# A perceiver block on Trainium2: first cross attention joined with the norm of its latents, and its 33 tail keys on two 64-row halves of TensorE

## The chip, the cores and the metric

One Trainium2 chip, one of its cores (core 0). A kernel's time is that of one launch of the whole program on the device, in microseconds. The kernel before took 2004.42 us in the median of three runs (2004.2 to 2007.45). Its profile is of a further execution, of 2006.4 us.

## The reference, cut to what matters

The program is a two-layer perceiver block in float32: cross attention, gated recurrence, a feed-forward layer, a second cross attention, self attention and a mixture of experts, each on a residual stream `x` of 128 batches x 32 latents x 128 features. The change touches the first cross attention alone:

```python
def _L0_xattn_ref(x, latents, mask, g1, b1, g2, b2, Wq, Wkv, Wout):
    heads, dim_head = (16, 64)
    xn = layer_norm(x, g1, b1)                 # context: 128 batches x 257 rows x 128
    ln_lat = layer_norm(latents, g2, b2)       # latents: 128 batches x 32 rows x 128
    q = ln_lat @ Wq
    kv = jnp.concatenate([xn, ln_lat], axis=1) @ Wkv    # 257 + 32 = 289 keys
    ...
    weight = jnp.where(full_mask, einsum('bhld,bhnd->bhln', q * scale, k * scale), neg)
    weight = softmax(weight)
    out = einsum('bhln,bhnd->bhld', weight, v)
    return out @ Wout
x = x + _L0_xattn_ref(ctx_1024, _layernorm(x), mask, g1, b1, g2, b2, Wq, Wkv, Wout)
```

So each batch has 289 keys: 256 context rows, the last context row, and its 32 latents. The last 33 are the *tail keys*. The latents are normalised twice, once outside and once by `layer_norm(latents, g2, b2)`.

## The kernel before

Stages follow one another, each a block of programs for the five engines (PE, DVE, ACT, POOL and SP, which issues the loads), with a barrier between blocks: `setup`, then `xattn0` (the stage of the change), and five more. Within a block the order of each engine's work is written out by hand, and engines meet at semaphores.

`xattn0` has three blocks. **First**, `ln_stats` (L74 to L133) makes mean and inverse deviations of all latents on DVE, with two square roots on ACT. **Second**, `xattn0_inputs` (L448) goes over the latents in 8 chunks of 512 rows, two buffers deep. For a chunk, DVE and ACT each normalise two of its four 128-row tiles (L480, L528), PE turns the four (L513), ACT copies the turned chunk into `latT` with gain and offset (L534), DVE multiplies by the gain (L486), POOL adds the offset (L501) and SP stores the chunk in DRAM (L557), from where it comes back as values. The last context rows go the same way at the end (`tailT`). **Third**, the attention proper. POOL first clears buffers (L681 to L686, all of `blocks` among them) while DVE, PE and SP wait for `zeroed`.

The attention runs in steps, one a batch, unrolled 8 deep (`run_steps`). Weights are folded: `A` takes the turned latents to queries in context space for each head, and `U` takes a head's weighted context to the output. In step s the engines work ahead by different distances. DVE takes statistics of batch s+7 (L755) and normalises s+6 (L762); POOL applies gain and offset (L694, L696); PE turns batch s+5 (L907), ACT and DVE split it into two float32r parts (L838, L786). PE makes queries for four heads (L879), ACT and DVE split them (L834, L773). PE makes the scores of batch s+3 for four head groups, three float32r products each (L853); DVE masks them and takes the largest (L728), ACT takes the exponentials (L801), DVE the inverse sums (L778). For batch s+2 ACT scales the probabilities (L809) and DVE turns them in 32x32 blocks, 256 keys in one instruction (L739), the tail keys in another (L741); SP then moves the blocks in four transfers so that keys lie on partitions (`probT`, L648), once PE is done with that buffer. For batch s PE makes the values: per 128 keys two float32 products of 256 columns, one for each pair of head groups (L863, two key tiles), then the same for the tail keys (L870). A float32 product is two records in the trace. ACT copies the result out (L819). Every fourth step PE projects the four finished batches with 16 products (L895), and DVE adds them to `x` (L782). A *tile* is four batches.

The tail keys' values lie in `a_tail`, 8 batches deep, on the 128 partitions: latent c on partition 4c, the last context row on partition 1, zeros elsewhere. SP loads a tile's tail in two transfers (L665, L667) every fourth step, and the product at L870 runs over all 128 rows. `LEAD` is 7: before the first batch there are seven steps, -7 to -1, in which only the work ahead is done.

Of the kernel before, what the change touches and what calls it, by code (L numbers as in the profile page):

```python
# [25 lines left out]
P = 128  # L26
# [47 lines left out]
def ln_stats(k, stack, name, extra=None):  # L74
# [11 lines left out]
    with nc.Block() as block:  # L86
# [41 lines left out]
        @block.scalar  # L128
        def _(act):
            for n, root in enumerate((rstd,) if extra is None else (rstd, twice)):  # L130
                act.wait_ge(inv_ready, n + 1)
                nc.scalar.activation(root[:], inv[:], ACT.Sqrt).then_inc(root_ready, 1)
    return (mean, rstd) if extra is None else (mean, rstd, twice)  # L133
# [314 lines left out]
def xattn0_inputs(k, io, stack):  # L448

    nc = k.nc
    k.latT = stack.enter_context(nc.sbuf_tensor("latT", [P, TOK], F32))
    k.tailT = stack.enter_context(nc.sbuf_tensor("tailT", [P, B], F32))
    with ExitStack() as st:
        z2 = st.enter_context(nc.sbuf_tensor("lat_z2", [P, 2, 4, D], F32))
        lat = st.enter_context(nc.sbuf_tensor("lat_affine", [P, 2, 4, D], F32))
        tail = st.enter_context(nc.sbuf_tensor("ctx_tail_affine", [P, 2, D], F32))
        bank = [st.enter_context(nc.psum_tensor(f"lat_ps{u}", [P, CH], F32)) for u in range(2)]
        tail_ps = st.enter_context(nc.psum_tensor("lat_ps_tail", [P, P], F32))
        z2_ready, z2_act, turned, copied = k.sem("lat_z2_ready"), k.sem("lat_z2_act"), k.sem("lat_turned"), k.sem("lat_copied")  # L460
        offset, offset_ready = st.enter_context(nc.sbuf_tensor("lat_offset", [P, TILES], F32)), k.sem("lat_offset_ready")
        scaled, affine_ready, stored = k.sem("lat_scaled"), k.sem("lat_affine_ready"), [k.sem(f"lat_stored{u}") for u in range(2)]
        tail_z, tail_scaled, tail_turned, tail_stored = (k.sem(f"ctx_tail_{n}") for n in ("z", "scaled", "turned", "stored"))
        spread = lambda a: a[:].unsqueeze(1).broadcast_to([P, 4, D])
        k.latents_stored = [(tail_stored, 16)] + [(sem, 16 * CHUNKS // 2 + 16) for sem in stored]
        mean, rstd, twice = ln_stats(k, st, "lat_ln", k.ctx_tail[:])
        with nc.Block() as block:

            @block.vector
            def _(dve):  # L470
                nc.vector.scalar_tensor_tensor(offset[:], mean[:, 0:TILES], -1.0, twice[:, 0:TILES], ALU.mult, ALU.mult).then_inc(offset_ready, 1)
                nc.vector.tensor_scalar(tail[:, 0, :], k.ctx_tail[:], mean[:, TILES:TILES + 1], rstd[:, TILES:TILES + 1],
                                        ALU.subtract, ALU.mult).then_inc(tail_z, 1)
                with dve.Fori(0, CHUNKS // 2) as g:
                    c = g * 2
                    for u in range(2):
                        dve.wait_ge(turned, c + (u + 1))
                        for j in range(2):
                            t = c * 4 + (4 * u + j)
                            last = nc.vector.tensor_scalar(z2[:, u, j, :], k.x[:, ds(t * D, D)], mean[:, ds(t, 1)],  # L480
                                                           twice[:, ds(t, 1)], ALU.subtract, ALU.mult)
                        last.then_inc(z2_ready, 1)
                        dve.wait_ge(stored[u], g * 16 + 16)
                        dve.wait_ge(z2_ready, c + (u + 1))
                        dve.wait_ge(z2_act, c + (u + 1))
                        nc.vector.tensor_tensor(lat[:, u], z2[:, u], spread(k.g2), ALU.mult).then_inc(scaled, 1)  # L486
                dve.wait_ge(tail_turned, 1)
                nc.vector.tensor_copy(k.tailT[:], tail_ps[:]).then_inc(tail_turned, 1)
                dve.wait_ge(tail_turned, 2)

            @block.gpsimd
            def _(pool):
                pool.wait_ge(tail_z, 1)
                nc.gpsimd.tensor_tensor(tail[:, 0, :], tail[:, 0, :], k.g1[:], ALU.mult).then_inc(tail_scaled, 1)
                pool.wait_ge(tail_scaled, 1)
                nc.gpsimd.tensor_tensor(tail[:, 1, :], tail[:, 0, :], k.b1[:], ALU.add).then_inc(tail_scaled, 1)
                with pool.Fori(0, CHUNKS // 2) as g:
                    c = g * 2
                    for u in range(2):
                        pool.wait_ge(scaled, c + (u + 1))  # L500
                        nc.gpsimd.tensor_tensor(lat[:, u], lat[:, u], spread(k.b2), ALU.add).then_inc(affine_ready, 1)  # L501

            @block.tensor
            def _(pe):
                pe.sem_inc(turned, 2)
                with pe.Fori(0, CHUNKS // 2) as g:
                    c = g * 2
                    for u in range(2):
                        pe.wait_ge(z2_ready, c + (u + 1))
                        pe.wait_ge(z2_act, c + (u + 1))  # L510
                        pe.wait_ge(copied, c + (u + 1))
                        for j in range(4):
                            last = nc.tensor.transpose(bank[u][:, j * P:(j + 1) * P], z2[:, u, j, :], k.ident[:])  # L513
                        last.then_inc(turned, 1)
                pe.wait_ge(tail_scaled, 2)
                nc.tensor.transpose(tail_ps[:], tail[:, 1, :], k.ident[:]).then_inc(tail_turned, 1)

            @block.scalar
            def _(act):
                act.sem_inc(copied, 2)  # L520
                act.wait_ge(offset_ready, 1)

                def normalise(c, u):

                    for j in range(2, 4):
                        t = c * 4 + (4 * u + j)
                        last = nc.scalar.activation(z2[:, u, j, :], k.x[:, ds(t * D, D)], ACT.Identity, bias=offset[:, ds(t, 1)],  # L528
                                                    scale=twice[:, ds(t, 1)])
                    last.then_inc(z2_act, 1)  # L530

                def copy(c, u):
                    act.wait_ge(turned, c + (u + 3))
                    nc.scalar.activation(k.latT[:, ds((c + u) * CH, CH)], bank[u][:], ACT.Identity, bias=k.b2c,  # L534
                                         scale=k.g2c).then_inc(copied, 1)

                for u in range(2):
                    normalise(0, u)
                with act.Fori(0, CHUNKS // 2 - 1) as g:
                    c = g * 2  # L540
                    for u in range(2):
                        copy(c, u)
                        act.wait_ge(scaled, c + (u + 1))
                        normalise(c + 2, u)
                for u in range(2):
                    copy(CHUNKS - 2, u)
                act.wait_ge(copied, CHUNKS + 2)

            @block.sync
            def _(sp):  # L550
                for u in range(2):
                    sp.sem_inc(stored[u], 16)
                with sp.Fori(0, CHUNKS // 2) as g:
                    c = g * 2
                    for u in range(2):
                        sp.wait_ge(affine_ready, c + (u + 1))
                        sp.dma_start(k.lat_dram[ds((c + u) * CH, CH), :].rearrange("(t p) d -> p t d", p=P),  # L557
                                     lat[:, u]).then_inc(stored[u], 16)
                sp.wait_ge(tail_scaled, 2)
                sp.dma_start(k.ctx_tail_dram, tail[:, 1, :]).then_inc(tail_stored, 16)  # L560

def xattn0(k, io):
# [3 lines left out]

    nc = k.nc
    with ExitStack() as stack:
        xattn0_inputs(k, io, stack)
# [56 lines left out]
        with nc.Block() as block:  # L630

            @block.sync
            def _(sp):
# [36 lines left out]
                for j in range(8 - LEAD):  # L670
                    load_raw(0, j)
# [1917 lines left out]
```

## Time and profile before

| | before |
|---|---|
| median of 3 runs | 2004.42 us (2004.2 to 2007.45) |
| profiled execution | 2006.4 us |
| its span, first to last instruction | 2004.6 us |
| PE / DVE / ACT / POOL busy, share of the span | 85% / 79% / 75% / 45% |
| `xattn0`: statistics of the latents begin | 39.0 us |
| chunks of the latents | 44.7 to 64.4 us |
| first score of the attention | 82.5 us |
| last product of the attention ends | 889 us |

The profile tells for each engine when it worked, on which line, how long, and what ended an idle time before. `x4` after a group is a number of records; the time beside it reaches from the start of the first to the end of the last. Records of PE overlap, since matmuls are pipelined: the time that one costs is the distance to the next one's start, not its own length.

### The profile page before, as it was taken

Reading aid. Unit: us, or ns where it says so; the run is one execution under the profiler, and the core shown is the slowest. Engines: PE = TensorE matmul, PEld = TensorE weight load, DVE = VectorE, ACT = ScalarE, POOL = GpSimd, SP = SyncE. Lnnn points to the kernel's source line nnn. Section 1 sums busy time; section 2 is a strip of 40 time slices with the busy share of each in tenths; the row PEclk is TensorE's granted clock in tenths of the full one; section 3 lists DMA queues with packets and bytes.
Section 4 is the critical chain, followed back from the end, with each engine's and each line's share of the span. In section 5 each row is a group of like instructions: output and inputs, shape, how many; then the busy total and the mean of one; then the engine's idle time right before and its main releaser. Section 6 shows DMA issues by size and latency. Waiting matters only on the chain. (4 is left out here: it accounts for less than half of the span.)

```text
span 2004.6 us, 51114 instructions
## 1 busy us (share of the span) xinstructions
PE 1702.9 (85%) x13415; PEld 1392.7 (69%) x13415; DVE 1590.9 (79%) x5000; ACT 1502.6 (75%) x4164; POOL 900.7 (45%) x1335
## 2 busy tenths in 40 slices
PE   3599999999999999973450479999999889979997
PEld 3499999999999999962340146666666656666775
DVE  4798888888888888845688778999999868876664
ACT  3588888888888888857485569999999778855553
POOL 1644444444444444404145314444444357725554
PEclk8699999999999999986575689999999989969999
DMA  4366666666666666630000029999999810015454
GB/s 140 96 171 162 160 162 161 161 161 162 160 160 160 160 160 160 153 93 0 0 0 0 0 69 243 250 251 250 247 244 250 212 33 0 1 25 101 99 98 104
DMA packets 224923, 261.66 MB, mean 131 GB/s; under 512 B 25144, under 2 KB 178268, under 8 KB 224720
## 3 DMA queue, kind: packets, MB, share of 16 engines
q1 hardware_dynamic: 223366, 258.64, 51.9%
q10 hardware_dynamic: 1194, 1.58, 0.3%
q0 software_dynamic: 288, 0.56, 0.1%
q8 instruction: 33, 0.54, 0.1%
q14 instruction: 42, 0.34, 0.1%
HBM read 88.19 MB, written 4.74 MB: 46 GB/s over the span
## 5 line engine op out<-in xcount | busy, mean ns | idle before, releaser
L801 ACT ACTIVATE a_prob<-a_neg,a_nmax 128x289 f32<-128x289 f32 x512 | 267.2, 527 | 1.2 <-DVE a_nmax L728 1.0
L863 PE MATMUL a_out<-a_probT,a_xn 128*128 128x256 f32 x1024 | 264.7, 382 | 3.5 <-DMA a_probT<-a_blocks 1.9
L694 POOL TENSOR_TENSOR a_xn<-a_z,g 128x256 f32<-128x256 f32 x128 | 94.1, 735 | 383.2 <-DVE a_z L762 383.2
L1686 ACT ACTIVATE b_prob<-b_neg,b_nmax 128x257 f32<-128x257 f32 x512 | 260.5, 514 | 5.6 <-DVE b_nmax L1621 5.0
L853 PE MATMUL a_score<-a_xnT,a_qT 128*128 128x290 f32 x1536 | 252.5, 314 | 1.1 <-DVE a_qT L773 1.1
L728 DVE CUSTOM_DVE_ANT_0 a_neg<-a_score,a_bias 128x289 f32<-128x289 f32 x512 | 211.0, 458 | 39.3 <-PE a_score L853 35.1
L809 ACT ACTIVATE a_prob<-a_prob,a_rinv 128x289 f32<-128x289 f32 x512 | 231.8, 529 | 1.7 <-DVE a_rinv L778 1.7
L853 PEld LDWEIGHTS a_score<-a_xnT,a_qT 128*128 128x128 f32 x1536 | 221.9, 190 | 8.0 <-issue 1.6
L1621 DVE CUSTOM_DVE_ANT_0 b_neg<-b_score,b_bias 128x257 f32<-128x257 f32 x512 | 188.8, 421 | 24.0 <-PE b_score L1791 16.8
L863 PEld LDWEIGHTS a_out<-a_probT,a_xn 128*128 128x128 f32 x1024 | 176.3, 192 | 18.6 <-issue 2.5
L739 DVE STREAM_TRANSPOSE a_blocks<-a_prob 128x1024 f32<-128x1024 f32 x128 | 159.4, 1246 | 23.5 <-ACT a_prob L809 16.9
L2357 POOL TENSOR_TENSOR m_hidden<-m_full,m_hidden 128x512 fp32r<-128x512 f32 (+1 forms) x88 | 114.2, 1298 | 109.6 <-ACT m_hidden L2316 109.5
L1632 DVE STREAM_TRANSPOSE b_blocks<-b_prob 128x1024 f32<-128x1024 f32 x128 | 156.8, 1225 | 2.7 <-DMA b_probT<-b_blocks 2.5
L879 PE MATMUL a_q<-latT,A 128*128 (+1 forms) x1024 | 139.8, 281 | 13.0 <-DVE a_qT L773 10.7
L879 PEld LDWEIGHTS a_q<-latT,A 128*128 128x128 f32 x1024 | 130.8, 196 | 14.9 <-DVE a_qT L773 12.1
L870 PE MATMUL a_out<-a_probT,a_tail 128*128 128x256 f32 x512 | 132.2, 381 | 0.0
L819 ACT ACTIVATE a_oT<-a_out 128x512 f32<-128x512 f32 x128 | 76.7, 599 | 71.6 <-PE a_out L870 71.6
L2311 ACT ACTIVATE m_silu<-m_g 128x512 f32<-128x512 f32 (+1 forms) x88 | 52.7, 598 | 91.1 <-PE m_g L2080 90.4
L895 PE MATMUL a_ctx<-U,a_oT 128*128 128x128 f32 x1024 | 119.7, 275 | 0.7 <-ACT a_oT L819 0.7
L895 PEld LDWEIGHTS a_ctx<-U,a_oT 128*128 128x128 f32 x1024 | 116.9, 192 | 1.1 <-ACT a_oT L819 1.1
L1592 POOL TENSOR_TENSOR b_last_part<-b_v_rows,b_prob 128x128 f32<-128x128 f32 x128 | 52.3, 408 | 129.5 <-ACT b_prob L1686 126.9
L870 PEld LDWEIGHTS a_out<-a_probT,a_tail 128*128 128x128 f32 x512 | 97.9, 191 | 13.5
(483 smaller groups left out, 4545.5 us busy)
## 6 DMA issues: line engine op xcount, KB each, us to landing
a_probT<-a_blocks SPq DMA_DIRECT2D x512, 192.0 KB, 3.5
b_probT<-b_blocks SPq DMA_DIRECT2D x256, 256.0 KB, 4.6
a_raw<-in_ctx SPq DMA_DIRECT2D x128, 128.0 KB, 3.0
b_raw<-in_ctx SPq DMA_DIRECT2D x64, 256.0 KB, 4.1
m_wide<-expert_weights SPq DMA_DIRECT2D x128, 128.0 KB, 6.6
a_kept<-keep SPq DMA_DIRECT2D x32, 257.0 KB, 3.4
b_kept<-keep SPq DMA_DIRECT2D x32, 257.0 KB, 4.7
b_v_rows<-ctx_tail_values SPq DMA_DIRECT2D x32, 256.0 KB, 4.8
```

What stands on the lines that cost most here:

```text
L728: nc.vector.tensor_tensor_reduce(out=neg[:, grp, :], in0=score_ps[grp][:, 0:KEYS0], in1=bias[:, n, :], scale=-DH0 ** -0.5, scalar=3.4e38, ...
L739: nc.vector.transpose(blocks[:, n, :, 0:2].rearrange("p r t g l -> p g r t l"), prob[:, n, :, 0:2 * P].rearrange("p g (r t c) -> p g r t c ...
L801: nc.scalar.activation(prob[:, par, grp, 0:KEYS0], neg[:, grp, :], ACT.Exp, bias=nmax[:, par, grp:grp + 1], scale=-1.0, accum_out=rsum[:, ...
L809: last = nc.scalar.activation(part, part, ACT.Copy, scale=rinv[:, j % 2, grp:grp + 1])
L853: last = nc.tensor.matmul(score_ps[grp][:, 0:even(KEYS0)], qT[:, a, un, bn, 4 * grp:4 * grp + 4, :], xnT[:, c, n, :], start=(p == 0), stop ...
L863: nc.tensor.matmul(out_ps[:, half, 0:2 * P], xn[:, j, kt, :], probT[:, u, 2 * half:2 * half + 2, kt, :], start=(kt == 0), stop=False)
L870: last = nc.tensor.matmul(out_ps[:, half, 0:2 * P], tail[:, j, :], probT[:, j % 2, 2 * half:2 * half + 2, 2, :], start=False, stop=True)
L879: last = nc.tensor.matmul(q_ps[:, h * P:(h + 1) * P], k.A[:, 4 * hg + h, :], k.latT[:, ds((t + ahead) * P, P)], start=True, stop=True)
L895: last = nc.tensor.matmul(proj_ps, oT[:, slot, :], k.U[:, slot % GROUPS * HG + slot // GROUPS, :], start=(slot == 0), stop=(slot == H - 1))
L1621: nc.vector.tensor_tensor_reduce(out=neg[:, par, grp, :], in0=score_ps[grp][:, 0:N_CTX], in1=bias[:, n, :], scale=-DH1 ** -0.5, scalar=3.4 ...
L1632: nc.vector.transpose(blocks[:, n, :, j % 2].rearrange("p r t g l -> p g r t l"), prob[:, j % 4, :, 0:2 * P].rearrange("p g (r t c) -> p g ...
L1686: nc.scalar.activation(prob[:, (j + 5) % 4, grp, :], neg[:, par, grp, :], ACT.Exp, bias=nmax[:, par, grp:grp + 1], scale=-1.0, accum_out=r ...
```

## The change

The block `xattn0_inputs` is gone, and its work stands at the head of the attention's block, unrolled over the 8 chunks; after chunks 1, 3, 5 and 7 each engine runs one of the steps -7 to -4 (`EARLY`), and `run_steps` goes on from -3. The loads of the first four raw batches and of the first mask, and POOL's clearing, move into the `ln_stats` block; only the third key tile of `blocks` is cleared. The chunk buffers are laid into `oT`, the turns into `out_ps`.

For the tail, latents 0 to 15 lie on partitions 4c, latents 16 to 31 on partitions 4c+1, the last context row on partition 2, and all of it stands twice, in partitions 0 to 63 and in 64 to 127. The values of head groups 0 and 1 are made from the lower half alone, those of groups 2 and 3 from the upper half. Heads are ordered in another way in `oT`, and `U` is indexed to match.

```diff
-def xattn0_inputs(k, io, stack):
...
+        EARLY = {1: 1, 3: 2, 5: 3, 7: 4}
+        z2, lat = oT[:, 0:8].rearrange("p (u t) d -> p u t d", u=2), oT[:, 8:16].rearrange("p (u t) d -> p u t d", u=2)
...
+        mean, root, twice = ln_stats(k, stack, "lat_ln", k.ctx_tail[:], first_loads, clear)
...  SP, tail loads of a tile
-                        sp.dma_start(tail[0:P:KEY_STEP, rows, :], k.lat_dram[ds((t + 2) * P, P), :].rearrange(
-                            "(b l) d -> l b d", l=L)).then_inc(tail_loaded[u], 16)
-                        sp.dma_start(tail[1:2, rows, :], k.ctx_tail_dram[ds((t + 2) * BPT, BPT), :].unsqueeze(0))\
+                        latents = k.lat_dram[ds((t + 2) * P, P), :].rearrange("(b l) d -> l b d", l=L)
+                        for first in (0, P // 2):
+                            for r in range(2):
+                                sp.dma_start(tail[first + r:first + P // 2:KEY_STEP, rows, :], latents[r * (L // 2):(r + 1) * (L // 2)])\
+                                    .then_inc(tail_loaded[u], 16)
+                        sp.dma_start(tail[2:P:P // 2, rows, :], k.ctx_tail_dram[batches, :].unsqueeze(0).broadcast_to([2, BPT, D]))\
                             .then_inc(tail_loaded[u], 16)
...  DVE, tail blocks of a batch
-                    nc.vector.transpose(blocks[:, n, 0:2, 2].rearrange("p r g l -> p g r l"),
-                                        prob[:, n, :, 2 * P:2 * P + 2 * L].rearrange("p g (r c) -> p g r c", c=L)).then_inc(blocks_ready, 1)
+                    for half in range(2):
+                        pair = slice(2 * half, 2 * half + 2)
+                        last = nc.vector.transpose(blocks[:, n, 0:3, 2, pair].rearrange("p r g l -> p g r l"), tail_windows(n, half))
+                    last.then_inc(blocks_ready, 1)
...  PE, tail values of a batch
-                        last = nc.tensor.matmul(out_ps[:, half, 0:2 * P], tail[:, j, :], probT[:, j % 2, 2 * half:2 * half + 2, 2, :],
-                                                start=False, stop=True)
+                        part = slice(half * (P // 2), (half + 1) * (P // 2))
+                        last = nc.tensor.matmul(out_ps[:, half, 0:2 * P], tail[part, j, :], probT[part, j % 2, :, 2, part], start=False, stop=True)
...  DVE, chunks of the latents and the steps between them
+                for c in range(CHUNKS):
...
+                    nc.vector.tensor_tensor(lat[:, u], z2[:, u], wide4(k.g2), ALU.mult).then_inc(lat_scaled, 1)
...
+                    if c in EARLY:
+                        step(-1, EARLY[c])
+                run_steps(dve, step, LEAD - len(EARLY), LAG)
```

`tail_windows(n, half)` reads three overlapping windows of 32 keys, 16 apart, of two head groups: 192 elements a partition.

## Rows read from the trace of the kernel before

**Rows 1.** Busy time by engine in stretches: start:end, length, each engine, PEclk, DMA
```profile
400.00:450.00 50.00, 50.00 (x339) 47.05 (x338) 43.07 (x157) 41.31 (x120) 23.73 (x46) 1.00 0.66 161
66.00:84.00 18.00, 10.66 (x42) 9.33 (x43) 7.79 (x29) 4.22 (x7) 14.44 (x26) 0.50 0.33 97
```
**Rows 2.** Timeline of PE, steady steps: start, length, engine, line, operation
```profile
407.56 1.97 PE L853 MATMUL a_score<-a_xnT,a_qT 128*128 128x290 f32 x12
409.37 1.05 PE L879 MATMUL a_q<-latT,A 128*128 x8
...
412.21 1.03 PE L870 MATMUL a_out<-a_probT,a_tail 128*128 128x256 f32 x4
412.89 2.00 PE L853 MATMUL a_score<-a_xnT,a_qT 128*128 128x290 f32 x12
...
418.24 1.96 PE L853 MATMUL a_score<-a_xnT,a_qT 128*128 128x290 f32 x12
...
420.93 3.74 PE L895 MATMUL a_ctx<-U,a_oT 128*128 128x128 f32 x32
...
427.12 1.15 PE L853 MATMUL a_score<-a_xnT,a_qT 128*128 128x290 f32 x6
```
**Rows 3.** Timeline of DVE: three rows of the lead-in, one of a steady step
```profile
88.43 0.45 DVE L728 CUSTOM_DVE_ANT_0 a_neg<-a_score,a_bias 128x289 f32<-128x289 f32 x1
...
91.26 0.40 DVE L741 STREAM_TRANSPOSE a_blocks<-a_prob 128x256 f32<-128x256 f32 x1
91.59 0.45 DVE L755 BATCH_NORM_STATS2 a_stats<-a_raw 128x6 f32<-128x128 f32 x2
...
93.65 0.45 DVE L728 CUSTOM_DVE_ANT_0 a_neg<-a_score,a_bias 128x289 f32<-128x289 f32 x1
...
407.53 0.69 DVE L773 TENSOR_TENSOR a_qT<-a_q,a_qT 128x512 fp32r<-128x512 f32 x1
```
**Rows 4.** Timeline of PE in the second cross attention, where tilings of the array alternate
```profile
1289.88 0.61 PE L1804 MATMUL b_v_ps<-wv1T,b_turned_in 128*128 128x128 f32 x4
1290.42 0.64 PE L1762 MATMUL b_out<-b_probT,b_v 128*32 128x128 f32 x16
1291.00 0.72 PE L1754 MATMUL b_score<-b_kT,b_qbd 32*128 32x257 f32 x8
1291.64 0.70 PE L1775 MATMUL b_k<-b_turned_in,wk1T 128*128 128x256 f32 x2
1292.18 0.38 PE L1783 MATMUL b_in<-ident,b_raw 128*128 128x128 f32 x2
```
**Rows 5.** Timeline of PE in setup, products on 64 rows, lower and upper half
```profile
26.73 0.27 PE L410 MATMUL setup_ps<-wk0T,wq0T 64*128 64x128 f32 x1
26.73 0.27 PE L410 MATMUL setup_ps<-wout,wv0T 64*128 64x128 f32 x1
```
**Rows 6.** Timelines of the chunks of the latents and of the first steps, four engines
```profile
47.09 1.55 DVE L480 TENSOR_SCALAR lat_z<-x,lat_ln_mean,lat_ln_twice 128x128 f32 x2
47.26 1.30 POOL L501 TENSOR_TENSOR lat_affine<-lat_affine,b 128x512 f32<-128x512 f32 x1 [0.95 <-DVE lat_affine L486]
48.73 0.69 DVE L486 TENSOR_TENSOR lat_affine<-lat_z,g 128x512 f32<-128x512 f32 x1
...
70.39 0.49 DVE L755 BATCH_NORM_STATS2 a_stats<-a_raw 128x6 f32<-128x128 f32 x2 [6.28 <-POOL a_bias L686]
71.90 2.08 PE L879 MATMUL a_q<-latT,A 128*128 128x128 f32 x8 [3.78 <-DVE a_qT L773]
74.02 0.60 ACT L834 ACTIVATE a_qT<-a_q 128x512 fp32r<-128x512 f32 x1 [5.26 <-PE a_q L879]
74.65 0.69 DVE L773 TENSOR_TENSOR a_qT<-a_q,a_qT 128x512 fp32r<-128x512 f32 x1 [1.12 <-ACT a_qT L834]
82.46 3.14 PE L853 MATMUL a_score<-a_xnT,a_qT 128*128 128x290 f32 x12 [1.08 <-DVE a_qT L773]
```
**Rows 7.** Timeline of SP's queue around the tail loads of a tile
```profile
421.68 0.66 SPq L665 DMA_DIRECT2D a_tail<-latents_normalised  x1
...
423.16 0.33 SPq L635 DMA_DIRECT2D a_raw<-in_ctx  x1
...
427.51 2.77 SPq L648 DMA_DIRECT2D a_probT<-a_blocks  x4
```

More of the change, by code:

```diff
@@ L71, in tile_stats, with ln_stats @@
     return k.nc.vector.bn_stats(k.stats[:, ds(t, 1), :], k.x[:, ds(t * D, D)])
[L74 removed]
+def ln_stats(k, stack, name, extra=None, sync=None, gpsimd=None):
     nc = k.nc
@@ L132, in _ @@
                 nc.scalar.activation(root[:], inv[:], ACT.Sqrt).then_inc(root_ready, 1)
+        if sync is not None:
+            block.sync(sync)
+        if gpsimd is not None:
+            block.gpsimd(gpsimd)
     return (mean, rstd) if extra is None else (mean, rstd, twice)
@@ L445, in live @@
     return not isinstance(g, int) or 0 <= 8 * g + j + ahead < n
-def xattn0_inputs(k, io, stack):
[L451 to L560, printed above, removed]
@@ L628, in q_half, with load_raw, load_kept, first_loads @@
             return qT[:, half, (j // 4 + ahead) % 2, :, 4 * hg:4 * hg + 4, :].rearrange("p b h l -> p h b l")
+        def load_raw(sp, g, j):
+            sp.dma_start(raw[:, j % 4], io["ctx_1024"][ds(g * 8 + j, 1), 0:2 * P, :].rearrange(
+                "b (p t) d -> p (b t) d", t=2)).then_inc(raw_loaded[j % 4], 16)
+        def load_kept(sp, t, u):
+            sp.dma_start(kept[:, u], k.keep0[ds(t * BPT, BPT), :].unsqueeze(0).broadcast_to([P, BPT, N_CTX])).then_inc(kept_loaded[u], 16)
+        def first_loads(sp):
+            for j in range(4):
+                load_raw(sp, 0, j)
+            load_kept(sp, 0, 0)
+        def clear(pool):
+            nc.gpsimd.memset(tail[:], 0.0)
+            nc.gpsimd.memset(prob[:, :, :, KEYS0:], 0.0)
+            nc.gpsimd.memset(blocks[:, :, :, 2], 0.0)
+            for half in (HI, LO):
+                nc.gpsimd.tensor_copy(xnT[:, half, :, KEYS0:], k.zero[:].unsqueeze(1).broadcast_to([P, 8, even(KEYS0) - KEYS0]))
+            nc.gpsimd.memset(bias[:, :, 2 * P:2 * P + L], 0.0).then_inc(zeroed, 1)
+        mean, root, twice = ln_stats(k, stack, "lat_ln", k.ctx_tail[:], first_loads, clear)
         with nc.Block() as block:
@@ L672, in _ @@
-                load_kept(0, 0)
-                for stored, count in k.latents_stored:
-                    sp.wait_ge(stored, count)
+                        batches = ds((t + 2) * BPT, BPT)
+                        latents = k.lat_dram[ds((t + 2) * P, P), :].rearrange("(b l) d -> l b d", l=L)
[3 more added lines that the diff above has]
+                                    .then_inc(tail_loaded[u], 16)
@@ L675, in _ @@
+                sp.wait_ge(z_ready, 1)
+                load_raw(sp, 0, 4)
+                sp.wait_ge(tail_stored, 16)
+                for u in range(2):
+                    sp.wait_ge(stored[u], CHUNKS // 2 * 16)
                 sp.wait_ge(zeroed, 1)
-                run_steps(sp, step, LEAD)
+                run_steps(sp, step, LEAD - 2)
             @block.gpsimd
             def _(pool):
-                nc.gpsimd.memset(tail[:], 0.0)
-                nc.gpsimd.memset(prob[:, :, :, KEYS0:], 0.0)
@@ L683, in _ @@
-                nc.gpsimd.memset(blocks[:], 0.0)
-                for half in (HI, LO):
-                    nc.gpsimd.tensor_copy(xnT[:, half, :, KEYS0:], k.zero[:].unsqueeze(1).broadcast_to([P, 8, even(KEYS0) - KEYS0]))
-                nc.gpsimd.memset(bias[:, :, 2 * P:2 * P + L], 0.0).then_inc(zeroed, 1)
                 spread = lambda a: a[:].unsqueeze(1).broadcast_to([P, 2, D])
@@ L862, in values @@
                     for half in range(2):
-                        nc.tensor.matmul(out_ps[:, half, 0:2 * P], xn[:, j, kt, :], probT[:, u, 2 * half:2 * half + 2, kt, :],
+                        nc.tensor.matmul(out_ps[:, half, 0:2 * P], xn[:, j, kt, :], probT[:, u, :, kt, half * (P // 2):(half + 1) * (P // 2)],
                                          start=(kt == 0), stop=False)
@@ L911, in step @@
                         tail_values(g, j)
-                run_steps(pe, step, LEAD, LAG)
+                pe.wait_ge(tail_scaled, 2)
+                nc.tensor.transpose(tail_ps, last_row[:, 1, :], k.ident[:]).then_inc(tail_turned, 1)
+                for c in range(CHUNKS):
+                    pe.wait_ge(z2_ready, c + 1)
+                    pe.wait_ge(z2_act, c + 1)
+                    wait(pe, lat_copied, c - 1)
+                    for j in range(4):
+                        last = nc.tensor.transpose(bank[c % 2][:, j * P:(j + 1) * P], z2[:, c % 2, j, :], k.ident[:])
+                    last.then_inc(lat_turned, 1)
+                    if c in EARLY:
+                        pe.wait_ge(lat_copied, c)
+                        step(-1, EARLY[c])
+                pe.wait_ge(lat_copied, CHUNKS)
+                pe.wait_ge(tail_copied, 1)
+                run_steps(pe, step, LEAD - len(EARLY), LAG)
     k.xattn0_weights.close()
```

92 lines of the change are left out of this document (73 added, 19 removed).

## The prediction, made before the changed kernel was run

> **What bounds the kernel now.** I read the table of stretches first. From 400 to 450 us PE is busy for 50.00 of 50.00 us, DVE for 43.07 and ACT for 41.31, at a granted clock of 1.00, its upper level of 2.4 GHz [rows 1]. PE is the bound there, and the other stretches between 150 and 850 us show the same. Then the timeline of PE: score to score takes 5.33 us in a plain step (407.56 to 412.89) and 8.88 in the step with the projection (418.24 to 427.12) [rows 2]. A tile of four batches thus takes 3 x 5.33 + 8.88 = 24.87 us.
>
> DVE is close behind. In the lead-in, where PE waits for it, DVE goes from mask to mask in 5.22 us (88.43 to 93.65) [rows 3]. That is its own floor for a plain step, 0.11 under PE's. Only the projection's step gives it room.
>
> Ahead of this lies a thin stretch. DVE waits 6.28 us for POOL's clearing until 70.39, and from there four steps of preparation take 12.07 us to the first score at 82.46 [rows 6]. From 66 to 84 us PE's granted clock is 0.50, the 1.2 GHz level [rows 1]. So two places decide: PE's work in 128 steps, and the time to the first score.
>
> **Part 1, the tail on two halves (PE).** The four records of the tail cost their distance: (1.03 - 0.38) / 3 = 0.216 each, where 0.38 is one record's length (four records of the 256-column kind span 1.03) [rows 2]. That is 0.86 us a batch. If the halves run together, two such distances stay: 0.43.
>
> Do they? In setup the products of one half start at 26.73, and so do those of the other [rows 5]. In the second cross attention eight records of 257 columns, two for each of four row groups, take 0.64 us from their start to the next line's (1291.00 to 1291.64) [rows 4]. One after another they would take 8 x 0.216 = 1.73; with all four groups side by side 2 x 0.216 = 0.43. So they do run side by side, and something costs 0.21 on top.
>
> That something is the change of the array's tiling. Three groups with changes stand in rows 4. L1804 (4 records of 128 columns at 0.11) takes 0.54 instead of 0.44: +0.10 ahead of the change. L1762 (16 records on four column groups, 4 x 0.11 = 0.44) takes 0.58: +0.14. L1754 is +0.21. L1775, the first on the whole array again, takes 0.54 instead of 0.43: +0.11. From L1804's start to L1783's it is 2.30 us against 1.74 without changes, so three changes cost 0.56, or 0.19 each. A tail on halves pays one on the way in and one on the way out: 0.43 + 2 x 0.19 = 0.81, against 0.86 now. Read segment by segment it is more: 0.14 before it, 0.64 itself and 0.11 after it, 0.89.
>
> The other end: the score's first record may hide its share, and if the way in costs 0.10 and the way out nothing more, the tail takes 0.74. So per batch between -0.12 and +0.03. I take 0.81, the mean of three changes in rows 4: -0.05 a batch. Over 128 batches that is -6 us, with ends -16 and +4.
>
> The Trainium skill, "TensorEngine Tiling (Array Packing)", Key Properties, says that a change of tiling mode, not of tile, drains TensorE. By that rule the gain is 0.43 less two drains; the trace agrees, with about 0.2 us each (L1754 and its neighbours). The rule speaks against this change, since each batch now changes twice and before not at all.
>
> **Part 2, the tail's blocks (DVE).** One instruction of 256 elements costs 0.33 us from its start to the next one's (91.26 to 91.59) [rows 3]. Two of 192 elements replace it. In proportion to elements each costs 0.25, and with no saving for size 0.33: together +0.17 to +0.33, I take +0.2. DVE's floor in a plain step rises from 5.22 to 5.42, over PE's 5.28. Its cover is the projection's step, where DVE now waits some 3 us in all (24.87 less 4 x 5.22 less about 0.6 for the addition to x and its statistics leaves 3.4 a tile). Over three plain steps DVE falls 3 x 0.14 = 0.4 us behind. Who waits for it first? PE's queries need the copy at L773: it ends at 408.22 and PE begins the queries at 409.37 [rows 2, 3]. The slack is 1.15 us, more than 0.4 + 0.2. So nothing reaches PE in the steady steps. In steps -2 to 0 and in the last one, where PE waits for DVE, the 0.2 counts: +0.8 us in all.
>
> **Part 3, five tail loads for two (SP).** One load of 32 rows x 4 batches is issued in 0.66 us [rows 7]. Four of half the size cost between 0.3 and 0.66 each, so the queue is busy 1 to 2 us longer, with the last load beside. Behind it stand the raw batch (423.16), the mask load and then the move of `probT` at 427.51 [rows 7]. Between the mask load's end near 424.1 and 427.51 the queue waits for PE anyway. The raw batch is used some 7 us later. This is free; without that cover it would cost up to 2 us x 32.
>
> **Part 4, latents and first steps together.** Gone: a block's end, POOL's clearing in DVE's way (it moves beside the statistics, where POOL is idle), and a separate run of four steps. Added: those steps between the chunks. A chunk's two L480 start at 47.09 and its L486 at 48.73, 1.64 us; alone the pair takes 0.6, but the second ends only with POOL's L501 (47.26 + 1.30) [rows 6].
>
> After a step POOL is idle again, so an even chunk takes 0.60 + 0.09 + 0.69 = 1.38. An odd one takes 1.64, and then the step's chain: four turns of 0.21 on PE at the low clock (0.85), queries to ACT's copy 2.12 (71.90 to 74.02), ACT to DVE 0.63, L773 0.69 [rows 6]. That is 4.29, so a pair takes 1.38 + 5.93 = 7.31 us. From 47.09: the first odd chunk ends at 53.0, the copy of `tailT` adds 0.3, three pairs add 21.9, and two steps also have L786 at 0.4 each: 76.0. The first score stands at 82.46 now, so -6.5 us. POOL's longer work in step -6 (about 5 us) may hold DVE's L480 for up to 1.3 in three chunks: then only -2.6. If the turns hide behind ACT's work it is -8.
>
> **Sum.** -6.5 - 6 + 0.8 = -11.7 us. The profiled execution took 2006.4 (span 2004.6 and 1.8 around it), the median of the runs is 2004.4. I count from the median: 2004.4 - 11.7 = 1993 us; a profiled execution would show 1995. The forecast's own range is 1981 (-8 - 16 + 0.6) to 2007 (-2.6 + 4 + 0.8).
>
> **Rivals.**
> *A, the halves cost no drain.* The tail takes 0.43, PE's plain step 4.90. Then DVE at 5.42 falls 0.5 behind a step, 1.5 a tile, the slack of 1.15 is used up, and PE waits about 0.4 a tile: -1.3 us x 32 = -42, with part 4: 1956 us. Rows 5 show the overlap, but there nothing changes tiling; rows 4 speak against. The Trainium skill, "TensorE: Matmul & The Clock Gate", Measured speedup vs the span model, gives a pack one matmul's time and about 4 ns a tile, with no drain; that would be this rival. Chance 0.08.
> *B, DVE becomes the bound.* If the lag of the plain steps is not made up, because the mask of the next tile starts late, three steps of four run at DVE's 5.42 instead of 5.33: 96 x 0.09 = +8.6 and no gain on PE: 2004.4 - 5.7 + 8.6 = 2007. For it: 0.11 us between the floors. Against: 3.4 us of room a tile. Chance 0.12.
> *C, slower: the two passes take turns.* A float32 product is two passes, and if the upper half's first waits for the lower half's second, three distances stay and two changes: 0.65 + 2 x 0.19 = 1.03 against 0.86, or +0.17 a batch. That is +22 us, and with -5.7 for the rest 2020 us. It decides from the point where a tail costs over 0.91, which eats part 4. Against it: L1754's eight records in 0.64 leave no room for turns. Chance 0.12.
> That the latents' part gains nothing is inside the forecast's range: its end -2.6 with -6 + 0.8 gives 1997.
>
> **How the numbers follow.** The forecast has 0.68, A 0.08, B 0.12, C 0.12. A difference of 0.2% (4 us) is about what a measurement of this kernel can tell from none. Of the forecast's 0.68, 0.60 lie under 2000.4 and 0.08 within 4 us of before; B lies on the upper edge and is split evenly. Faster: 0.60 + 0.08 = 0.68. Same: 0.08 + 0.06 + 0.02 = 0.16. Slower: 0.12 + 0.04 = 0.16. The range leaves out A and C: 1978 to 2009.
>
> **What would show it.** First score near 76 us instead of 82.46. L870 as records of 64 rows, in pairs that start within 0.02 us, 0.3 us from pair to pair, and 0.8 us from the first to a score that runs freely. Score to score about 5.28 in plain steps, PE still busy all the time, and DVE's wait for scores at the start of a tile shorter. Two L741 of about 0.3 each. I am wrong if PE shows idle time before L879 or L863 (B or A), if four L870 starts are 0.2 apart (C), or if the first score comes after 80.

## The result, and the profile after

The changed kernel takes 2031.54 us (median of 4 runs, 2029.69 to 2033.27), against 2004.31 us for the kernel before (4 runs, 2002.31 to 2007.45). The ratio is 1.0135, 95% interval 1.0120 to 1.0149: slower by 27 us where 12 us less were forecast. The profiled execution took 2030.97 us, with a span of 2029.2. Two executions that took far longer than all others of the same kernel (3494 us of the kernel before, 5463 us in experiment 10) are in no median and no ratio of this text.

First the table of stretches of the changed kernel, the same two stretches as in [rows 1] (start:end, length, busy time of PE, PEld, DVE, ACT and POOL, PEclk, DMA share, GB/s).

```profile
400.00:450.00 50.00, 47.75 (x326) 40.87 (x327) 42.07 (x158) 40.13 (x118) 22.01 (x43) 1.00 0.65 160
66.00:84.00 18.00, 13.45 (x75) 12.56 (x74) 14.04 (x42) 10.80 (x26) 12.24 (x16) 0.71 0.37 103
```

PE, busy for 50.00 of 50 us before, is now idle for 2.25, and no other engine is busier for it. The clock is not the reason in this stretch: 1.00 as before. So something new holds PE up. Its timeline (start, length, engine, line, operation, and in brackets the idle time ahead and who ended it) shows where:

```profile
398.67 1.87 PE L828 MATMUL a_score<-a_xnT,a_qT 128*128 128x290 f32 x12
...
401.26 3.74 PE L870 MATMUL a_ctx<-U,a_oT 128*128 128x128 f32 x32
404.84 1.03 PE L838 MATMUL a_out<-a_probT,a_xn 128*128 128x256 f32 x4
408.12 0.41 PE L882 MATMUL a_ctx<-ident,a_xn 128*128 128x128 f32 x2 [2.25 <-DVE x L719]
...
409.95 1.89 PE L828 MATMUL a_score<-a_xnT,a_qT 128*128 128x290 f32 x12
...
414.61 0.70 PE L846 MATMUL a_out<-a_probT,a_tail 64*128 64x256 f32 x4
415.25 1.88 PE L828 MATMUL a_score<-a_xnT,a_qT 128*128 128x290 f32 x12
...
428.40 3.74 PE L870 MATMUL a_ctx<-U,a_oT 128*128 128x128 f32 x32
453.09 3.74 PE L870 MATMUL a_ctx<-U,a_oT 128*128 128x128 f32 x32
480.11 3.74 PE L870 MATMUL a_ctx<-U,a_oT 128*128 128x128 f32 x32
504.80 3.74 PE L870 MATMUL a_ctx<-U,a_oT 128*128 128x128 f32 x32
```

The plain step is 5.30 and 5.28 us, as forecast. But from projection to projection it is 27.14, 24.69, 27.02 and 24.69 us: every second tile is late. From 150 to 850 us a tile took 24.83 to 24.89 before. In the late one PE waits at L882 for VectorE's addition to `x` at L719.

VectorE's timeline goes one step further back:

```profile
399.35 0.16 DVE L715 RECIPROCAL a_rinv<-a_rsum 128x4 f32<-128x4 f32 x1
399.43 0.39 DVE L723 TENSOR_TENSOR a_xnT<-a_ctx,a_xnT 128x256 fp32r<-128x256 f32 x1
402.82 0.46 DVE L657 CUSTOM_DVE_ANT_0 a_neg<-a_score,a_bias 128x289 f32<-128x289 f32 x1 [3.00 <-issue]
...
405.51 0.59 DVE L678 STREAM_TRANSPOSE a_blocks<-a_prob 128x192 f32<-128x192 f32 x2
406.03 0.44 DVE L692 BATCH_NORM_STATS2 a_stats<-a_raw 128x6 f32<-128x128 f32 x2
```

VectorE stands still for 3.00 us ahead of the mask at L657, and the releaser is "issue": the engine waits for nothing that the profile shows. PE's score for that mask had been running since 398.67 (first row of the fence before). The gap stands right behind the branch that closes the loop over the batches (`run_steps`, L441), which ends a pass of eight batches, two tiles. The view of waits (engine, line, releaser: us in total, times, longest) counts these gaps from 150 to 850 us:

```profile
DVE a_neg L657 <- issue: 39.2, 13, 3.8
...
PEld a_ctx L882 <- issue: 34.4, 13, 3.4
PE a_ctx L882 <- DVE x L719: 29.6, 13, 3.0
...
ACT a_prob L758 <- DVE a_nmax L657: 25.7, 13, 2.7
```

Thirteen gaps, one for each return to the loop's start, and the waits of PE and ACT behind them thirteen times too. The same view of the kernel before has none of the four. What VectorE waits for is suggested by the page's list of queues (packets, MB, share). It has two queues that carry instructions. I take q14 for VectorE's: in the experiments below its count changes with edits of VectorE's program alone. In the page of the changed kernel:

```profile
q14 instruction: 108, 0.88, 0.2%
```

and in the page before:

```profile
q14 instruction: 42, 0.34, 0.1%
```

Each packet is 8 KB (0.88 MB over 108). The 66 additional packets lie in the loop: the DMA view from 250 to 800 us shows 51 packets on this queue in the changed kernel and none in the kernel before. That is about five a pass (13 x 5 = 65): each pass fetches its instructions again. And two packets start at this gap, one just ahead of it and one in it, in the same view from 399.5 to 402.9 us:

```profile
q14 instruction: 2, 0.02, 2.2%
```

The lead-in came out ahead of the forecast:

```profile
74.91 3.24 PE L828 MATMUL a_score<-a_xnT,a_qT 128*128 128x290 f32 x12 [1.08 <-DVE a_qT L710]
```

The first score stands at 74.91 against 82.46 [rows 6], with 76.0 forecast. The granted clock of 66:84 is 0.71 instead of 0.50 [rows 1]: PE works there instead of waiting.

### The profile page after: what moved, and what is told of

The parts are those of the page before. It is cut to its first block and busy times, and to the rows that moved or that the text cites. A ratio compares the mean times of both kernels' runs of the same rounds, so it can differ in the third digit from the quotient of the medians.

```text
span 2029.2 us, 51269 instructions
## 1 busy us (share of the span) xinstructions
PE 1703.9 (84%) x13415; PEld 1327.3 (65%) x13415; DVE 1605.3 (79%) x5128; ACT 1509.2 (74%) x4164; POOL 897.8 (44%) x1335
## 5 line engine op out<-in xcount | busy, mean ns | idle before, releaser
L657 DVE CUSTOM_DVE_ANT_0 a_neg<-a_score,a_bias 128x289 f32<-128x289 f32 x512 | 210.2, 456 | 84.3 <-issue 43.6
L828 PE MATMUL a_score<-a_xnT,a_qT 128*128 128x290 f32 x1536 | 246.4, 310 | 2.9 <-DVE a_qT L710 2.9
L828 PEld LDWEIGHTS a_score<-a_xnT,a_qT 128*128 128x128 f32 x1536 | 215.7, 194 | 45.5 <-issue 45.5
L1675 ACT ACTIVATION_READ_ACCUMULATOR b_prob<-b_neg,b_nmax 128x1 f32 x512 | 104.2, 204 | 0.0
L1900 POOL TENSOR_TENSOR s_spread<-s_keys,head_of_feature 128x1536 f32<-128x1536 f32 x32 | 88.8, 2776 | 34.7 <-ACT s_keys L1994 34.7
```

The source lines that it names most:

```text
L657: nc.vector.tensor_tensor_reduce(out=neg[:, grp, :], in0=score_ps[grp][:, 0:KEYS0], in1=bias[:, n, :], scale=-DH0 ** -0.5, scalar=3.4e38, ...
L828: last = nc.tensor.matmul(score_ps[grp][:, 0:even(KEYS0)], qT[:, a, un, bn, 4 * grp:4 * grp + 4, :], xnT[:, c, n, :], start=(p == 0), stop ...
L1675: nc.scalar.activation(prob[:, (j + 5) % 4, grp, :], neg[:, par, grp, :], ACT.Exp, bias=nmax[:, par, grp:grp + 1], scale=-1.0, accum_out=r ...
```

## The experiments

**1. Only the place moved.** Forty increments of a semaphore that nobody waits for, ahead of VectorE's first wait in setup, where it waits for `x` anyway:

```diff
             def _(dve):
+                pad = k.sem("pad")
+                for _ in range(40):
+                    dve.sem_inc(pad, 1)
                 dve.wait_ge(x_loaded, 16)
```

> The changed kernel with 40 one-instruction semaphore increments put at the start of DVE's setup program, where DVE waits for x anyway; nothing else differs. It moves DVE's loop over the batches from instruction 429-711 of its program to 469-751. Theory P (place): the changed kernel loses time because DVE's loop reaches a few instructions into a fourth 128-instruction block of its program, so that each pass of the loop fetches its instructions anew; 13 of 14 passes then take 27.0 to 28.7 us for the tile at the loop's end instead of 24.7, 38 us in all. Moved by 40, the loop lies in three blocks: no such tiles, q14 back near 50 packets, 2031.5 - 38 = 1993 us (+-4). Theory L (length): a loop of 283 instructions is too long wherever it stands: 2031 us. Theory D (data): the stall comes from the five tail loads or the two turns of the tail, and the fetches go with it: 2031 us.

Measured: 1992.68 us (5 runs, 1989.06 to 1994.02), ratio to the kernel before 0.9931 (0.9917 to 0.9944). In its page and its view of stretches:

```profile
q14 instruction: 43, 0.35, 0.1%
```

```profile
400.00:450.00 50.00, 50.00 (x343) 43.06 (x343) 44.28 (x167) 42.30 (x123) 23.44 (x45) 1.00 0.67 165
```

PE is busy throughout again: all 27 distances from projection to projection between 150 and 850 us are 24.68 to 24.70, and the waits of PE and ACT are gone. Forty instructions more in the program, and 39 us less: the place of the loop was the whole of the loss. (In the profiled executions 1.3 of the 39 us lie ahead of the loop: the first score stands at 73.6 instead of 74.9.) This is the version that beats both kernels.

**2. The kernel before, moved the bad way.** The same edit with 25 increments puts its untouched loop at 440 to 714.

> The kernel before with 25 such increments in the same place; its loop of 275 instructions moves from 415-689 to 440-714, past the end (711) at which the changed kernel's loop stalls. Theory P: every second tile takes 27 to 29 us instead of 24.9, DVE stands idle about 3 us after its loop's branch, q14 has some 65 packets more, and the time is 2004 + 38 = about 2042 us. Theories L and D: 2004.5 us, since neither length nor data differ.

Measured: 2077.67 us (4 runs), ratio 1.0349 (1.0325 to 1.0372), 108 packets. None of the change's work is in this kernel. The direction is shown, the size was missed: +72 us for the +38 expected, where the changed kernel loses 39 to its twin. VectorE's timeline shows two stalls a pass instead of one:

```profile
421.20 0.46 DVE L731 CUSTOM_DVE_ANT_0 a_neg<-a_score,a_bias 128x289 f32<-128x289 f32 x1 [2.92 <-issue]
...
422.35 0.08 DVE L731 DVE_READ_ACCUMULATOR2_ANT a_nmax<- 128x1 f32 x1
423.48 0.46 DVE L731 CUSTOM_DVE_ANT_0 a_neg<-a_score,a_bias 128x289 f32<-128x289 f32 x1 [1.05 <-issue]
```

The second one, between the third mask and the fourth, lies between instructions 451 and 454 of my count. The clock has a part in the +72 too; see below.

**3 and 4. The two parts alone.** In 3 the tail on halves with its five loads in the kernel before (VectorE's loop at 425 to 707), in 4 the merge of the latents with the old tail (419 to 693). The diffs are the two parts of the one shown with the change.

> The kernel before with the tail's part of the change alone (two halves of TensorE, two turns of 192 elements, five tail loads); latents and clearing stay in their own blocks. DVE's loop is 283 instructions at 425-707. Theory P: no stall if the block ends between 708 and 711, then 2004.3 - 6 + 0.8 = 1999 us by the prediction's own terms; if it ends between 690 and 707, 2037 us. Theories L and D: 2037 us.

> The changed kernel with the tail's part undone (one product over 128 rows, one turn of 256 elements, two tail loads); latents' norm stays merged with the attention. DVE's loop is 275 instructions at 419-693. All three theories: no stall, and the merge's own gain, 6.5 us by the prediction (7.5 to 9 by the changed kernel's trace): 1995 to 1998 us. If it comes out over 2004, the merge itself costs time in a place that I have not seen.

Measured on one chip with the two above (the kernel before 2006.05, 15 runs): the tail alone 1999.47 us, ratio 0.9970 (0.9957 to 0.9983), the merge alone 1995.06, ratio 0.9949 (0.9937 to 0.9962). Each part alone is a gain, and neither loop is fetched again (43 and 42 packets). The tail alone has the very loop of 283 instructions that loses 39 us in the changed kernel, only four instructions earlier. That rules the length out, and it excludes the halves, the two turns and the five loads as the loss.

The first score of the merge alone:

```profile
73.85 1.54 PE L822 MATMUL a_score<-a_xnT,a_qT 128*128 128x290 f32 x5 [1.08 <-DVE a_qT L704]
```

**5 to 8. Is it a block of 128, and where is its edge?** The edit of experiment 1 with 128, 168, 20 and 28 increments.

> The changed kernel with 128 more semaphore increments at the start of VectorE's program: its loop over the batches stands at instructions 557 to 839 in place of 429 to 711. Place in blocks of 128 instructions (my theory; the fetches move 8 KB, 128 instructions of 64 B): the loop stands in its blocks exactly as in the changed kernel, over four of them, so it is fetched again in every pass: about 108 packets of instructions, tiles alternating 24.7 / 27 to 29 us, 2029 to 2034 us. Rival, any filler helps (something in the start of the program, or in how the engines start, not the place): as with 40 of them, 1990 to 1995 us and 43 packets. Rival, blocks of 256 instructions: moved by half a block, 1990 to 1995 us as well.

> The changed kernel with 168 increments (loop at 597 to 879), one block of 128 past the one with 40 increments. Place in blocks of 128: the loop lies over three blocks, no fetch inside it, all tiles 24.69 to 24.70 us, 1990 to 1995 us. If 128 increments alone cost time at the start, first score later than 74.9 us and the span longer by just that. Blocks of 256: half a block from a place that was good, so it could stall, about 2030 us.

> The changed kernel with 20 increments: loop at 449 to 731. With a block's edge between 453 and 455, as the kernels run so far bound it, only 4 to 6 of the loop's instructions stand ahead of the edge, and 21 to 23 in the fourth block: still fetched again in every pass. Place: over 2025 us, 108 packets or so, and, if the stall grows with what stands in the fourth block, as in the kernel before with 25 increments (5 to 12 behind the edge at each end, 2078 us), more than the changed kernel's 2031 us. Rival, only the fetches' number counts: 2031 us.

> The changed kernel with 28 increments: loop at 457 to 739, wholly behind the edge between 453 and 455. Place: three blocks, no fetch inside the loop, 43 packets or so, tiles 24.69 to 24.70 us, 1990 to 1995 us, although it is only eight instructions from the kernel with 20. Rival, the stall fades with distance: between the two.

| increments | loop at | instruction packets | time, us |
|---|---|---|---|
| 0 (the change) | 429 to 711 | 108 | 2031.54 |
| 20 | 449 to 731 | 108 | 2084.56 |
| 28 | 457 to 739 | 43 | 1993.16 |
| 40 | 469 to 751 | 43 | 1992.68 |
| 128 | 557 to 839 | 109 | 2030.76 |
| 168 | 597 to 879 | 44 | 1996.15 |

The rows with 20, 28 and 168 are one run each, the one with 128 is 4 (ratio 1.0123, 1.0107 to 1.0140). All four came out by *place* (1996.15 us is a little over the 1990 to 1995 expected). A shift by 128 brings the loss back to the microsecond, so the pattern repeats with 128: blocks of 256 and "any filler helps" are out. Blocks of 64 would fit these times as well; for 128 speak the packets of 8 KB, with 64 bytes an instruction (the working is under "Why the prediction was wrong"). Eight instructions, from 20 to 28, are worth 91 us. The waits with 128 increments have the same row as the changed kernel's:

```profile
DVE a_neg L660 <- issue: 38.7, 13, 3.7
```

With 20 increments the loop has only three instructions ahead of the edge, and VectorE stands still twice, 5.4 us in all. Its timeline there:

```profile
412.36 0.40 DVE L726 TENSOR_TENSOR a_xnT<-a_ctx,a_xnT 128x256 fp32r<-128x256 f32 x1
414.97 0.46 DVE L660 CUSTOM_DVE_ANT_0 a_neg<-a_score,a_bias 128x289 f32<-128x289 f32 x1 [2.21 <-issue]
418.59 0.08 DVE L660 DVE_READ_ACCUMULATOR2_ANT a_nmax<- 128x1 f32 x1 [3.17 <-issue]
```

The second gap falls between a mask and the read of its accumulator, and again the profile names no engine as its cause; each of the two gaps has a packet of q14 in it (DMA view, 412.8 to 414.9 and 415.5 to 418.5 us). By my count the second is between instructions 451 and 452, which fits experiment 2, so I put the edges at 452 + 128 n. (The expectation still had 453 to 455.) The kernel before, the changed one and experiments 1 to 8 all agree: those whose loop starts before 452 and reaches 708, or both 128 later, stall, the others do not. The changed kernel's loop starts 23 instructions ahead of the edge and shows no second gap; presumably their work covers the second fetch. At 12 ahead (experiment 2) the second gap is 1.05 us, at 3 ahead 3.17. Over 14 passes the loss is 2.8 us a pass with 23 ahead, 5.1 with 12 and 6.6 with 3.

These losses are not VectorE's gaps alone. With 20 increments PE, having waited 5.00 us for VectorE until 423.77, goes on at a granted clock of 0.50, the 1.2 GHz level, until 430 us (its timeline, and stretches as above):

```profile
423.77 0.66 PE L885 MATMUL a_ctx<-ident,a_xn 128*128 128x128 f32 x2 [5.00 <-DVE x L722]
```

```profile
418.80:423.30 4.50, 0.00 (x0) 0.00 (x0) 4.44 (x17) 2.68 (x9) 0.59 (x1) 0.99 0.26 90
423.30:430.00 6.70, 6.23 (x21) 4.77 (x22) 1.93 (x10) 3.04 (x8) 1.76 (x4) 0.50 0.18 35
```

The stretch from 150 to 850 us of the changed kernel, of experiment 2 and of the one with 20 increments, in this order:

```profile
150.00:850.00 700.00, 670.41 (x4505) 572.71 (x4504) 588.15 (x2204) 561.00 (x1612) 313.70 (x592) 0.99 0.64 157
150.00:850.00 700.00, 653.52 (x4246) 609.03 (x4245) 538.65 (x1967) 520.73 (x1507) 294.30 (x554) 0.96 0.60 145
150.00:850.00 700.00, 640.78 (x4174) 542.42 (x4173) 544.72 (x2038) 519.50 (x1488) 290.58 (x550) 0.95 0.59 145
```

PE is idle for 30, 46 and 59 us. A mean clock of 0.99, 0.96 and 0.95 takes some 7, 28 and 35 us of full speed from the 700 (an estimate from these rows). The sums, 37, 75 and 94 us, are close to the losses of 39, 72 and 92. So in the two kernels with a second gap over a third of the loss is PE's clock, which fell after the longer waits. In the changed kernel it fell behind 4 of the 13 gaps; those late tiles take 28.7 us, where most others take 27.0 to 27.2.

**9. What is the overlap of the halves worth?** On experiment 1's kernel, both pairs of head groups take the lower 64 rows. The upper pair's sums are then wrong; only the time is read:

```diff
-    last = nc.tensor.matmul(out_ps[:, half, 0:2 * P], tail[part, j, :], probT[part, j % 2, :, 2, part], start=False, stop=True)
+    last = nc.tensor.matmul(out_ps[:, half, 0:2 * P], tail[low, j, :], probT[low, j % 2, :, 2, part], start=False, stop=True)
```

> The changed kernel with 40 increments, and the products of the tail for both pairs of head groups read the lower 64 rows (the upper pair's tail is computed from the wrong rows; everything else as it was). It asks what running side by side is worth. The halves run side by side (my step for the tail: 0.43 instead of 0.86): with both on one half the four records take four distances, 0.43 us more a batch, so a plain step of 5.71 instead of 5.28 and 1992.7 + 128 x 0.43 = 2048 us. The halves take turns (rival C of the prediction, which priced turns at 0.65): 0.22 more at most, 2020 us or less. No overlap at all, the gain of the tail came from something else: 1993 us as it is.

Measured: 2048.6 us (4 runs, 2044.51 to 2053.77), ratio to the kernel before 1.0217 (1.0189 to 1.0245). PE's timeline:

```profile
399.88 1.88 PE L831 MATMUL a_score<-a_xnT,a_qT 128*128 128x290 f32 x12
...
404.53 1.13 PE L850 MATMUL a_out<-a_probT,a_tail 64*128 64x256 f32 x4
405.59 1.88 PE L831 MATMUL a_score<-a_xnT,a_qT 128*128 128x290 f32 x12
```

The step is 5.71, the tail takes 1.06 to the next line's start instead of 0.64 (414.61 to 415.25). Two distances of 0.21 are saved by running side by side. Rival C, passes that take turns, is out.

**10. What does the tail cost as a whole, and what lies under it?** Experiment 1's kernel without the tail's products on PE, so that its sums lack the tail, the last product of the values raising `out_ready`:

```diff
-    for half in range(2):
-        part = slice(half * (P // 2), (half + 1) * (P // 2))
-        last = nc.tensor.matmul(out_ps[:, half, 0:2 * P], tail[part, j, :], probT[part, j % 2, :, 2, part], start=False, stop=True)
-    last.then_inc(out_ready, 1)
```

> The changed kernel with 40 increments, without the tail's products on PE (the tail's part is missing from the sums over values); loads, turns and VectorE's work as they were. It gives the whole price of the tail on PE with its changes of tiling, and VectorE's floor. My steps: PE's plain step falls by 0.81 to 4.47, so VectorE (5.42 a plain step, 22.3 a tile with the addition to x and its statistics) becomes the bound: tiles of 22.3 to 23.2 us instead of 24.69, plain steps near 5.4 where PE waits for VectorE, and 1992.7 - 31 x (1.5 to 2.4) = 1918 to 1946 us. Rival A/B reading, VectorE is already level with PE and its lag isn't made up in the projection's step: tiles of 24.2 or more, over 1975 us.

Measured: 1959.68 us (median of 3 runs, 1959.07 to 1960.10), ratio 0.9778 (0.9757 to 0.9799), above the 1918 to 1946 that I had expected. PE's timeline:

```profile
396.08 3.74 PE L871 MATMUL a_ctx<-U,a_oT 128*128 128x128 f32 x32
...
401.79 1.97 PE L831 MATMUL a_score<-a_xnT,a_qT 128*128 128x290 f32 x12
...
406.26 1.94 PE L831 MATMUL a_score<-a_xnT,a_qT 128*128 128x290 f32 x12
...
410.69 1.96 PE L831 MATMUL a_score<-a_xnT,a_qT 128*128 128x290 f32 x12
413.37 1.16 PE L855 MATMUL a_q<-latT,A 128*128 x8 [0.72 <-DVE a_qT L713]
...
416.13 1.94 PE L831 MATMUL a_score<-a_xnT,a_qT 128*128 128x290 f32 x12
...
419.79 3.74 PE L871 MATMUL a_ctx<-U,a_oT 128*128 128x128 f32 x32
```

Where PE runs freely its step is 4.43 (406.26 to 410.69); the one before it, from 401.79, is 4.47. So the tail on halves costs 5.28 - 4.45 = 0.83 us, and the old one 5.33 - 4.45 = 0.88. Where PE waits for VectorE's L713, the step is 5.44 (410.69 to 416.13), VectorE's floor. The tile takes 23.71 us (396.08 to 419.79), more than the 22.3 to 23.2 that I had expected. The projection's step is why: VectorE doesn't run through it freely. It waits in it 1.01 us for ACT's copy of the turned batch and 0.39 for the score:

```profile
401.73 0.42 DVE L726 TENSOR_TENSOR a_xnT<-a_ctx,a_xnT 128x256 fp32r<-128x256 f32 x1 [1.01 <-ACT a_xnT L798]
...
402.74 0.46 DVE L660 CUSTOM_DVE_ANT_0 a_neg<-a_score,a_bias 128x289 f32<-128x289 f32 x1 [0.39 <-PE a_score L831]
```

## Why the prediction was wrong

**The step that failed** is the sum of part 2: "So nothing reaches PE in the steady steps." It priced VectorE's instructions by their length and not by their number and their place in the program. The two parts together add 14 instructions ahead of the loop and 8 inside it, and with that the loop's end moved over the edge at 708 while its start stayed ahead of the one at 452. That costs 38.9 us (2031.54 to 1992.68): VectorE stands still for some 3 us at each return to the loop's start, PE waits 29.6 us for it from 150 to 850 us, and some 7 us more, by the estimate above, go to PE's clock. Without it the kernel takes what was forecast. No term of the sum stood for it, and no rival: B, which has VectorE as the bound, is a lag of 0.09 a step, and the plain steps don't show it. The trace before did show what was to be asked: its list of queues has a line of instruction packets, and its loop needed none of them. What it can't show is how near the loop was to the edge; that takes a count of the instructions of both kernels.

The Trainium skill, "Runtime: NRT & Kernel Launch", Instruction fetch mechanics, says that a taken branch to a target outside the window of two pages forces a fetch and a stall; on that the trace agrees, with 3.00 us behind the loop's branch at 399 us. It gives blocks of 16 KiB, 256 instructions, though, which makes 64 bytes each. By blocks of 256 the shift by 128 would not have brought back 2030.76 us, and the packets would not be 8 KB: here the runs decide against 256. Nor do two pages of 128 fit: the kernel before jumps back over three such blocks, with no packet from 250 to 800 us.

Point by point, by the runs without the stall:

- *Part 1, the tail:* 0.81 forecast, 0.83 measured (experiment 10), of which 0.42 are the two distances (experiment 9 less experiment 1). The remaining 0.41 I put down to the two changes of tiling, against 2 x 0.19; no run has the changes alone. (The Trainium skill, "TensorEngine Tiling (Array Packing)", Key Properties: a change of tiling mode drains the array. The trace agrees in that each seems to cost 0.2 us; it doesn't show the drain itself.) Per batch -0.05 forecast; a plain step went from 5.33 to 5.28 and a tile from 24.87 to 24.69, -0.045 a batch. Right. The old tail cost 0.88, so that the gain is a difference of two nearly equal numbers, and rival A, with no drain, is out.
- *Part 2, VectorE's turns:* from L678's start to L692's it is 0.52 (405.51 to 406.03) against 0.33 [rows 3], so +0.19 for +0.2. Its floor in a plain step is 5.44 for 5.42. PE's 50.00 of 50 us in experiment 1 show that this is hidden, as said. Rival B is out.
- *Part 3, the tail loads:* no wait for them stands in the waits of experiment 1 or of the changed kernel. Free, as said.
- *Part 4, the merge:* first score at 74.91, 7.55 earlier for 6.5 forecast, within the ends. It stands at 73.85 in the merge alone, 8.6 earlier, past the better end of -8. Too careful. The merge alone gives -11.0 us, 2.4 more than its first score; where these come from is open.
- *The sum:* 2004.4 - 11.7 = 1993 was forecast, and 1992.68 is what the kernel takes when its loop fits. That the two agree to 0.3 us is partly luck, since the merge alone gave 11.0 for 6.5. The two parts measured alone add up to -6.6 - 11.0 = -17.6, both together gave -13.4. With intervals of some 2.5 us on each of the three I can't call the 4 us between them an effect. The tail alone should give 4.9 by its own trace (128 x 0.045 = 5.8 less a first score that stands 0.9 later, at 83.34), and 6.6 is within its interval of that.
- *The chances:* "B lies on the upper edge and is split evenly" gives 0.08 + 0.06 = 0.14 for the same and 0.12 + 0.06 = 0.18 for slower. The prediction has 0.16 for each and gives no reason for the 0.02 moved.
- *What would show me wrong:* "I am wrong if PE shows idle time before L879 or L863 (B or A)". PE's idle time did come, but before the turns at L882 (L907 of the kernel before), so even this list looked for VectorE's lag in the wrong place.
- *Rival A's price:* 1956 for a tail of 0.43. Without any tail on PE the kernel takes 1959.68 (experiment 10), so 1956 was too low: I had let VectorE run freely through the projection's step.

How the fetch works inside is inferred: the runs show the edges, the packets and the gaps. Why a loop over three blocks stays while one over four does not (how many blocks are kept, and whether the next is fetched ahead) was not separated. That the gaps in VectorE's work are waits for these fetches rests on the packets at them and on their coming and going with the loop's place.

## What to carry to other kernels

Before pricing an edit of a loop written out for a busy engine, count that engine's instructions from its program's start to the loop's two ends, and compare the page's instruction packets and any "issue" gap behind the loop's branch after the edit. Here 22 instructions more on VectorE turned a gain of 0.7% into a loss of 1.35%. If packets appear inside the loop, shift it with a few idle instructions ahead of it, where the engine waits anyway; here that was worth 39 us. (A shorter loop was not tried.) Look at TensorE's granted clock behind such gaps too: here it fell, and made the longer ones dearer. And before taking work off the bound, measure the next engine's floor with that work left out: here even a free tail would have ended near 1960.

## What the runs showed that I had not expected

- A loop of 283 VectorE instructions costs nothing or up to 92 us in 14 passes (1992.68 to 2084.56), by where it starts; with 275 instructions the kernel before can be made 72 us slower without touching its loop. Over a third of the 92 and of the 72 us is PE's granted clock at 0.50 after waits of 4 to 5 us.
- Forty idle semaphore increments at the start of the program don't show in the end: 1992.68 us for the 1993 forecast without them. With 168 the one run took 1996.15 us, over the highest of the five with forty (1994.02), so that these may cost some 2 us.
- A change of TensorE's tiling seems to cost 0.2 us on PE's critical path (0.41 for two, by difference), and it can eat a halved row count: the halves save 0.42 of distance and give 0.41 back. What is left is 0.045 a batch by the tiles; rows of two decimals don't tell where it comes from.
